# Attention layers of a decoder kernel: the split maxima moved within SBUF instead of through DRAM, and the stacks issued behind them

## The chip, the core and the metric

One core of one Trainium2 chip runs the whole decoder in one launch. The metric is the device time in microseconds (us), median of three runs. The engines are named as the profile names them: PE is TensorE (PEld its weight loads), DVE is VectorE, ACT is ScalarE, POOL is GpSimd, and SP is SyncE, which issues almost all DMAs of this kernel, in the order of one list.

## The reference, cut to what matters

Two decoder layers over `x` of shape (16, 256, 256): attention with rotary positions and a causal mask, cross attention over 120 context rows, an expert layer by product keys, a second self-attention with a band added to its scores, a bidirectional attention flow, and a mixture of experts. The change touches the three attention layers, which all have 16 heads of 16 dims:

```python
scores = jnp.einsum('bhqd,bhkd->bhqk', Q, K) / sqrt(d)      # + causal mask, or + band
probs = jax.nn.softmax(scores, axis=-1)
heads = jnp.einsum('bhqk,bhkd->bhqd', probs, V)
```

## The kernel before

`attention_stage` is one program that is built three times, as `causal`, `cross` and `band`. Each works through 16 batch elements of 256 queries. One batch element is called b, and its 16 heads fall in two halves of 8 (`CH` = 8), named by c = 0 and c = 1.

For each b the stage does this. The projections of queries and keys are made in four jobs (`project`, j = 0 to 3: queries and keys of half 0, then of half 1). Each result is split into three bf16 parts that sum to the fp32 value. SP writes the parts to DRAM (`qscratch` L467, three transfers; `kscratch` L470, one) and reads them back laid out by head: one transfer into `qs` (L481) and three into `ks` (L483). These four reads are the **stack** of one half, `stack(b, par, c)`. Six slots of 16 rows, 96 rows in all, let one bf16 matmul give an fp32-like score.

The scores are computed twice. `find` (L584) makes them with queries on the partitions, and DVE takes each query's negated maximum (`nmax`, L840 or L843). When the 8 heads of a half are found, `turn_max(b, par, c)` transposes the maxima on PE (L598); ACT copies them (L713, L714); POOL splits them into three bf16 parts with three operations (L769, L770, L772, the last signals `n_ready`). SP stores the parts in DRAM (L489), waits for the landing, and reads them into rows 96 to 98 of `qs` (L491). `head` (L608) makes the scores again with keys on the partitions, and these three rows, times ones in `ks`, subtract the maximum in the same matmul. ACT applies exp (L707, `probT`), PE multiplies by the values (L628), ACT copies the result to `oq` (L723), and SP gathers `oq` into `oqp` with 2 times 4 transfers (L500, in `weigh` with j = 2 and 3). The first copy to `oq` of the next b waits until those gathers have landed. Row sums, reciprocals and the output projection follow (L639, L861, L864, L645, L871, L655, L880).

Every engine walks the same written order, `macro(e, b, par)` (L330): a loop over s = 0 to 15, in which `head(b, s)` and `find(b + 1, s)` go side by side, and the other work has fixed places. A macro therefore works on b (heads), b + 1 (find, values), b + 2 (turn, project, stack of half 0) and b - 1 (sums, out). What concerns the change:

- at s = 0, after `head(b, 0)`: `stack(b + 1, 1)`, then `turn_max(b, 1)`, and at the end of the step `find(b + 1, 0)`
- at s = 2: the second gather of b - 1 (`weigh` with j = 3), and projection 0
- at s = 8: `stack(b + 2, 0)`, then projection 2
- at s = 9: `turn_max(b + 1, 0)`, after `find(b + 1, 9)`
- at s = 11: projection 3; at s = 14: the first gather of b

`stack` exists on SP alone; the other engines pass over it. PE's `find` of head 0 or 8 waits until the stack of its half has landed (`stacked[c]`), and PE's `head` 0 or 8 waits for the maxima of its half (`n_in[c]`). So `find(b + 2, 0)`, at the start of the next macro, needs the stack issued at s = 8, and `head(b + 1, 0)`, just before it in PE's order, needs the maxima sent at s = 9. Between these two on PE stands the transpose L598 of `turn_max(b + 1, 1)`.

Of the kernel before, what the change touches and what calls it, by code (L numbers as in the profile page):

```python
# [11 lines left out]
BF16 = mybir.dt.bfloat16  # L12
# [4 lines left out]
B, S, D = 16, 256, 256  # L17
# [10 lines left out]
def wait(eng, sem, value):  # L28

    if isinstance(value, int) and value <= 0:  # L30
        return
    eng.wait_ge(sem, value)
# [20 lines left out]
class Room:  # L53
# [12 lines left out]
    def sb(self, name, shape, dt=F32):  # L66
        return self.ctx.enter_context(self.nc.sbuf_tensor(f"{self.stage}_{name}", shape, dt))
# [4 lines left out]
    def sem(self, name):  # L72
        self.sems.append(self.nc.alloc_semaphore(f"{self.stage}_{name}"))
        return self.sems[-1]
# [104 lines left out]
def attention_stage(nc, kind, stats, ident, d, ahead, context):  # L179
# [19 lines left out]
    CH = HEADS // DC  # L199
# [7 lines left out]
    ROWS = 6 * HD  # L207
# [11 lines left out]
    with ExitStack() as ctx:  # L219
        r = Room(nc, ctx, kind)  # L220
        stats.open(r)
        sb, ps, sem = r.sb, r.ps, r.sem
# [36 lines left out]
        qs = sb("qs", [P, 2, HEADS, S], BF16)  # L259
# [5 lines left out]
        npart = sb("npart", [CH, 2, 3, S], BF16)  # L265
# [5 lines left out]
        warm = sb("warm", [P, 1])  # L271
        qscratch = nc.dram_tensor(f"{kind}_qscratch", (2, DC, 6, P, S), BF16).ap()
        kscratch = nc.dram_tensor(f"{kind}_kscratch", (2, DC, 3, P, KS), BF16).ap()
        nscratch = nc.dram_tensor(f"{kind}_nscratch", (2, 2, 3, CH, S), BF16).ap()

        ps_p = ps("ps_p", [P, 2, 512])
        ps_1 = ps("ps_1", [P, 2, 512])
# [20 lines left out]
        n_taken = sem("n_taken")  # L298
        n_rest = sem("n_rest")
        n_ready = sem("n_ready")  # L300
        n_out = sem("n_out")
        n_in = [sem(f"n_in{c}") for c in range(DC)]
        s2_done = sem("s2_done")
        p_ready = sem("p_ready")
# [16 lines left out]
        def there(b):  # L321

            return 0 <= b < B


        PROJECT, OUT, VALUES, STACK = (2, 5, 8, 11), 13, 15, 8
        WEIGH, SUMS, NORMALISE, MOMENTS, NORM = 6, 4, 7, 3, 4
        MOVES = 16 * HEADS // 2

        def macro(e, b, par):  # L330

            for s in range(HEADS):
                e.head(b, par, s)
                if s > 0:
                    e.factor(b, par, s - 1)
                if s == 0:
                    if there(b + 1):
                        e.stack(b + 1, 1 - par, 1)
                    if there(b - 1):
                        e.turn_max(b, par, 1)  # L340
                if there(b - 1):
                    if s == WEIGH - 4:
                        e.weigh(b - 1, 1 - par, NQUAD - 1)
                    if s == SUMS:
                        e.sums(b - 1, 2 * b + 2)
                    if s == SUMS + 1:
                        e.sums_end(b - 1)
                    if s == NORMALISE:
                        e.normalise(b - 1, 1 - par)
                if s >= WEIGH and s % 4 == WEIGH % 4:  # L350
                    e.weigh(b, par, (s - WEIGH) // 4)
                if s == NORM and there(b + 3):
                    e.norm(b + 3)
                if there(b + 2):
                    if s == 1:
                        e.turn(b + 2, par)
                    if s == 2:
                        e.bias(b + 2)
                    if s == STACK:
                        e.stack(b + 2, par, 0)  # L360
                    if s in PROJECT:
                        e.project(b + 2, par, PROJECT.index(s))
                if s == OUT and there(b - 1):
                    e.out(b - 1)
                if s == MOMENTS and there(b - 2):
                    e.moments(b - 2)
                if there(b + 1):
                    if s == VALUES:
                        e.values(b + 1, 1 - par)
                    e.find(b + 1, 1 - par, s)  # L370
                    if s == CH + 1:
                        e.turn_max(b + 1, 1 - par, 0)
            e.factor(b, par, HEADS - 1)
            e.end()

# [52 lines left out]
        def _(sp):  # L428
# [25 lines left out]
            def settle(sem, value):  # L454


                wait(sp, sem, value)
                sp.wait_ge(weights, 16 * nload)

            class Sync(Part):  # L460
# [25 lines left out]
                def turn_max(self, b, par, c):  # L486

                    settle(n_ready, 2 * b + c + 1)
                    sp.dma_start(nscratch[par, c].rearrange("a h t -> h a t"), npart[:, c, :, :]).then_inc(n_out, 16)  # L489
                    settle(n_out, 16 * (2 * b + c + 1))  # L490
                    sp.dma_start(qs[ROWS:ROWS + 3, par, c * CH:(c + 1) * CH, :], nscratch[par, c]).then_inc(n_in[c], 16)  # L491

                def weigh(self, b, par, j):

# [18 lines left out]
        def _(pe):  # L513
# [12 lines left out]
            class Tensor(Part):  # L526
# [73 lines left out]

                def head(self, b, par, h):
                    if h % CH == 0:
                        pe.wait_ge(n_in[h // CH], 16 * (b + 1))

                    wait(pe, p_ready, HEADS * b + h - 1)
                    for k in range(KT):
                        c0, n = kcol[k], S - qfrom[k]
                        mm = nc.tensor.matmul(ps_2[0:KN, h % 2, c0:c0 + n], ks[0:ROWS + 3, par, h, k * KN:(k + 1) * KN],  # L608
                                              qs[0:ROWS + 3, par, h, qfrom[k]:S], start=True, stop=not rope)
                        if rope:  # L610
                            mm = nc.tensor.matmul(ps_2[:, h % 2, c0:c0 + P], ident16[:], mask[:, 1, :],  # L611
                                                  start=False, stop=True)
                    mm.then_inc(s2_done, 1)
# [47 lines left out]
        def _(act):  # L661
# [5 lines left out]
            class Scalar(Part):  # L667
# [41 lines left out]
                def turn_max(self, b, par, c):  # L709
                    act.wait_ge(nt_done, 2 * b + c + 1)  # L710
                    wait(act, n_ready, 2 * b + c - 1)
                    wait(act, n_out, 16 * (2 * b + c - 1))
                    nc.scalar.activation(nfull[:, c, :], ps_n[0:CH, 0:S], ACT.Copy)  # L713
                    nc.scalar.activation(npart[:, c, 0, :], ps_n[0:CH, 0:S], ACT.Copy).then_inc(n_taken, 1)  # L714

# [1733 lines left out]
def decoder(nc, d):  # L2449
    with ExitStack() as ctx:  # L2450
        def sb(name, shape):
            return ctx.enter_context(nc.sbuf_tensor(name, shape, F32))
        stats = Stats(nc, sb)
        ident = sb("ident", [P, P])
        ahead = Ahead(nc, ctx)
        with ExitStack() as early:
            context = Context(nc, early, "early")
            attention_stage(nc, "causal", stats, ident, d, ahead, context)
            attention_stage(nc, "cross", stats, ident, d, ahead, context)
        peer_stage(nc, stats, ident, d, ahead)  # L2460
        last = Last(nc, ctx, "last")
        attention_stage(nc, "band", stats, ident, d, ahead, last)
        route = Route(nc, ctx.enter_context(ExitStack()))
        bidaf_stage(nc, stats, ident, d, route, last)
        moe_stage(nc, ident, d, route)
# [13 lines left out]
```

## Time and profile before

| | us |
|---|---|
| median of 3 runs (3632.45 to 3639.7) | 3635.33 |
| the profiled execution | 3634.44 |
| its span, first to last instruction | 3632.6 |
| causal stage, about | 31 to 511 |
| cross stage, about | 515 to 895 |
| expert layer by product keys, about | 895 to 2392 |
| band stage, about | 2392 to 2830 |

Over the whole span the page of the profile gives PE 89% busy, DVE 72%, POOL 57%, ACT 51%, and a mean granted TensorE clock of 0.948 of full speed. In the 40 slices of the page, the slices 6 to 9 (the cross stage) show PE at 7 to 8 tenths with a clock of 8 to 9 tenths, while causal and band show PE at 8 to 9 tenths with the clock at 9. A row of the timeline reads: start, duration, engine, line, operation, out<-in, and in brackets the idle time of the engine before it with what ended it. Where operations of a kind follow one another, x3 says that three are merged in the row.

### The profile page before, as it was taken

How to read it: one execution, taken by the hardware profiler on the slowest of the kernel's cores; microseconds unless marked ns; L12 is line 12 of the kernel's file. 1: busy time of each engine (PE TensorE's matmuls, PEld its weight loads, DVE VectorE, ACT ScalarE, POOL GpSimd, SP SyncE). 2: the span in 40 equal slices, each digit the busy share in tenths (PEclk: the TensorE clock that was granted, in tenths of full speed). 3: DMA queues.
4: the chain of work that ended last, by engine and by line, in shares of the span. 5: the costliest groups of instructions: out<-in, count | busy, mean ns of one | idle time of the engine just before them, and what ended most of it. 6: DMA issues, size and time to landing. Idle time of an engine off the chain costs nothing. (4 is left out here: it accounts for less than half of the span.)

```text
span 3632.6 us, 95157 instructions
## 1 busy us (share of the span) xinstructions
PE 3238.9 (89%) x33694; PEld 2753.6 (76%) x33695; DVE 2620.0 (72%) x10695; ACT 1834.9 (51%) x4800; POOL 2067.8 (57%) x2454
## 2 busy tenths in 40 slices
PE   5999977876599999999999999978888898899998
PEld 4777754554589999999999999855555686899998
DVE  6666634453899999999999999848888577333333
ACT  1434434543577777777777777726565221222221
POOL 4444435552377777777777777758886232333332
PEclk8999988997799999999999999989999898899999
DMA  5444424442200000000000000035553231566665
GB/s 155 111 118 125 109 66 119 122 116 74 84 2 2 2 2 2 2 2 2 3 2 2 2 3 2 2 82 128 138 131 88 84 100 44 170 185 177 186 176 134
DMA packets 255744, 277.73 MB, mean 76 GB/s; under 512 B 43871, under 2 KB 200287, under 8 KB 254815
## 3 DMA queue, kind: packets, MB, share of 16 engines
q1 hardware_dynamic: 241694, 253.40, 24.1%
q0 software_dynamic: 13632, 18.91, 3.6%
q8 instruction: 245, 4.01, 0.5%
q14 instruction: 173, 1.41, 0.1%
HBM read 187.34 MB, written 72.29 MB: 71 GB/s over the span
## 5 line engine op out<-in xcount | busy, mean ns | idle before, releaser
L1295 POOL TENSOR_TENSOR peer_hot_v<-peer_hot_e,peer_parts 80x512 bf16<-80x512 bf16 x768 | 920.9, 1226 | 271.0 <-DVE peer_hot_e L1338 266.2
L1091 PE MATMUL peer_ps_u<-peer_up,peer_g 128*128 128x256 f32 x2048 | 513.8, 396 | 0.6 <-DVE x_all L1438 0.6
L1072 PEld LDWEIGHTS peer_ps_h<-peer_xnT,peer_down 128*128 128x128 f32 x4096 | 503.9, 195 | 13.6 <-DMA peer_down<-in_peer_down 1.0
L1072 PE MATMUL peer_ps_h<-peer_xnT,peer_down 128*128 128x128 f32 x4096 | 505.9, 278 | 0.7 <-DMA peer_down<-in_peer_down 0.7
L1201 ACT ACTIVATE peer_hot_u<-peer_count,peer_minus_u 80x128 bf16<-80x128 bf16 x1536 | 462.3, 426 | 2.6 <-PE peer_ps_w L1082 1.5
L1082 PE MATMUL peer_ps_w<-peer_hot_v,peer_hot_u 80*128 80x32 bf16 x12288 | 348.3, 177 | 80.9 <-DVE peer_g L1352 36.1
L1091 PEld LDWEIGHTS peer_ps_u<-peer_up,peer_g 128*128 128x128 f32 x2048 | 382.5, 197 | 49.5 <-issue 1.0
L1082 PEld LDWEIGHTS peer_ps_w<-peer_hot_v,peer_hot_u 80*128 80x128 bf16 x12288 | 338.1, 97 | 101.2 <-issue 64.6
L2272 POOL DMA_INDIRECT out<-moe_y,moe_target x71 | 112.5, 1585 | 312.6 <-DVE moe_y L2371 309.6
L1169 ACT ACTIVATE peer_g<-peer_ps_h 128x512 f32<-128x512 f32 x256 | 145.3, 590 | 249.4 <-PE peer_ps_h L1072 249.1
L2216 PE MATMUL moe_ps_t<-moe_xgT,moe_w 128*128 128x128 f32 x2272 | 267.9, 277 | 0.0
L2216 PEld LDWEIGHTS moe_ps_t<-moe_xgT,moe_w 128*128 128x128 f32 x2272 | 262.0, 194 | 0.1
L2226 PE MATMUL moe_ps_y<-route_w,moe_hT 128*128 x1136 | 256.8, 379 | 0.0
L2226 PEld LDWEIGHTS moe_ps_y<-route_w,moe_hT 128*128 128x128 f32 x1136 | 210.5, 190 | 25.7
L1344 DVE TENSOR_TENSOR peer_hot_u<-peer_count,peer_uvT 80x2048 bf16<-80x2048 bf16 x160 | 229.9, 1437 | 0.0
L707 ACT ACTIVATE causal_probT<-causal_ps 128x384 f32<-128x384 f32 x256 | 124.5, 488 | 204.3 <-PE causal_ps L611 201.3
L2252 ACT ACTIVATE moe_hT<-moe_hT 128x512 f32<-128x512 f32 x142 | 89.4, 629 | 229.4 <-DVE moe_hT L2362 229.4
L843 DVE TENSOR_REDUCE band_nmax<-band_ps 128x2 f32<-128x512 f32 x256 | 171.6, 680 | 41.9 <-PE band_ps L584 41.3
L840 DVE TENSOR_REDUCE causal_nmax<-causal_ps 128x1 f32<-128x128 f32 (+1 forms) x512 | 153.0, 349 | 58.2 <-PE causal_ps L588 57.8
L1206 ACT ACTIVATE peer_hot_u<-peer_hot_u,peer_iota 80x2048 bf16<-80x2048 bf16 x96 | 192.2, 2002 | 3.1
L1352 DVE TENSOR_TENSOR peer_g<-peer_ps_w,peer_g 128x512 f32<-128x512 f32 x256 | 173.9, 679 | 11.8 <-PE peer_ps_w L1082 11.8
L707 ACT ACTIVATE band_probT<-band_ps 128x512 f32<-128x512 f32 x256 | 146.9, 593 | 64.2 <-PE band_ps L608 59.9
(373 smaller groups left out, 7235.0 us busy)
## 6 DMA issues: line engine op xcount, KB each, us to landing
moe_w<-in_moe_w SPq DMA_DIRECT2D x142, 512.0 KB, 4.5
causal_qs<-causal_qscratch SPq DMA_DIRECT2D x32, 384.0 KB, 3.9
cross_qs<-cross_qscratch SPq DMA_DIRECT2D x32, 384.0 KB, 3.6
band_qs<-band_qscratch SPq DMA_DIRECT2D x32, 384.0 KB, 4.0
route_w<-in_moe_w SPq DMA_DIRECT2D x8, 1024.0 KB, 6.0
causal_qscratch<-causal_part SPq DMA_DIRECT2D x32, 192.0 KB, 2.7
causal_kscratch<-causal_part SPq DMA_DIRECT2D x32, 192.0 KB, 2.0
causal_ks<-causal_kscratch SPq DMA_DIRECT2D x32, 192.0 KB, 4.2
```

The source lines that it names most:

```text
L707: nc.scalar.activation(probT[0:KN, h, :], ps_2[0:KN, h % 2, 0:COLS], ACT.Exp).then_inc(p_ready, 1)
L843: ins = nc.vector.tensor_reduce(nmax[:, :, h], ps_1[:, h % 2, 0:TT * KS].rearrange("p (q k) -> p q k", q=TT), AX.X, ALU.max, negate=True)
L1072: mm = nc.tensor.matmul(ps_h[:, n % 2, k * P:(k + 1) * P], down[:, c, 4 * n + k, :], xnT[:, par, c, :], start=(c == 0), stop=(c == DC - 1))
L1082: mm = nc.tensor.matmul(ps_w[:, n % 2, k * EV:(k + 1) * EV], hot_u[0:SEL, n % RING, k // 2, :, k % 2], hot_v[0:SEL, n % RING, part, k // 2 ...
L1091: mm = nc.tensor.matmul(ps_u[:], g[:, par, v, :], up[:, v, :], start=(v == 0), stop=(v == EV - 1))
L1201: ins = nc.scalar.activation(hot_u[0:SEL, n % RING, k // 2, :, k % 2], count[0:SEL, :, 0], ACT.Square, bias=minus_u[0:SEL, token:token + 1])
L1206: nc.scalar.activation(flat, flat, ACT.Relu, bias=iota[0:SEL, 1:2], scale=-1.0).then_inc(u_act_ready, 1)
L1295: ins = nc.gpsimd.tensor_tensor(hot_v[0:SEL, n % RING, part], hot_e[0:SEL, n % RING], w, ALU.mult)
L1344: nc.vector.tensor_tensor(hot_u[0:SEL, n % RING], numbers.broadcast_to((SEL, CHUNK // 2, P, 2)), ut, ALU.is_equal).then_inc(u_ready, 1)
L1352: nc.vector.tensor_tensor(gs, ps_w[:, n % 2, :].rearrange("p (k v) -> p v k", v=EV), gs, ALU.mult).then_inc(gw_ready, 1)
L2216: mm = nc.tensor.matmul(ps_h[:, half, m * P:(m + 1) * P], w1[:, par, half, c, m * P:(m + 1) * P], xgT[:, par, c, :], start=(c == 0), stop= ...
L2226: mm = nc.tensor.matmul(ps_y[:, par, 0:D], hT[:, par, m, :], w2[:, ex, m, :], start=(m == 0), stop=(m == HC - 1))
```

## The change

The scratch tensor `nscratch` and the semaphore `n_out` go. The three parts of the maxima are moved by three transfers within SBUF, each from 8 partitions of `npart` (512 bytes each) to one row of `qs`; `n_in[c]` counts three transfers, and ACT's wait before it overwrites `npart` is on `n_in[c]` in place of `n_out`. In `macro`, `turn_max(b, 1)` now stands ahead of `stack(b + 1, 1)` at s = 0, and `stack(b + 2, 0)` moves from s = 8 to the end of s = 10, behind `turn_max(b + 1, 0)`.

```diff
-        PROJECT, OUT, VALUES, STACK = (2, 5, 8, 11), 13, 15, 8
+        PROJECT, OUT, VALUES, STACK = (2, 5, 8, 11), 13, 15, CH + 2
...
                 if s == 0:
+                    if there(b - 1):
+                        e.turn_max(b, par, 1)
                     if there(b + 1):
                         e.stack(b + 1, 1 - par, 1)
-                    if there(b - 1):
-                        e.turn_max(b, par, 1)
...
-                    if s == STACK:
-                        e.stack(b + 2, par, 0)
...
                     if s == CH + 1:
                         e.turn_max(b + 1, 1 - par, 0)
+                if s == STACK and there(b + 2):
+                    e.stack(b + 2, par, 0)
...
                 def turn_max(self, b, par, c):
 
                     settle(n_ready, 2 * b + c + 1)
-                    sp.dma_start(nscratch[par, c].rearrange("a h t -> h a t"), npart[:, c, :, :]).then_inc(n_out, 16)
-                    settle(n_out, 16 * (2 * b + c + 1))
-                    sp.dma_start(qs[ROWS:ROWS + 3, par, c * CH:(c + 1) * CH, :], nscratch[par, c]).then_inc(n_in[c], 16)
+                    for k in range(3):
+                        row = ROWS + k
+                        sp.dma_start(qs[row:row + 1, par, c * CH:(c + 1) * CH, :], npart[:, c, k, :]).then_inc(n_in[c], 16)
...
-                        pe.wait_ge(n_in[h // CH], 16 * (b + 1))
+                        pe.wait_ge(n_in[h // CH], 3 * 16 * (b + 1))
...
-                    wait(act, n_out, 16 * (2 * b + c - 1))
+                    wait(act, n_in[c], 3 * 16 * b)
```

## Rows read from the trace of the kernel before

**Rows 1.** Waits of PE, cross stage: who <- whom: us in total, times, longest

```profile
PE cross_ps L608 <- DMA cross_qs<-cross_nscratch: 35.2, 16, 5.6
PE cross_ps L608 <- ACT cross_probT L707: 10.4, 8, 2.8
```

**Rows 2.** Waits of PE, band stage

```profile
PE band_ps_n L598 <- DVE band_nmax L843: 15.7, 16, 1.0
...
PE band_ps L608 <- DMA band_qs<-band_nscratch: 1.6, 1, 1.6
```

**Rows 3.** Timeline of SP, one macro of the cross stage and the next stack

```profile
718.42 0.29 SPq L489 DMA_DIRECT2D cross_nscratch<-cross_npart  x1
720.11 0.25 SPq L491 DMA_DIRECT2D cross_qs<-cross_nscratch  x1
...
728.50 2.50 SPq L500 DMA_DIRECT2D cross_oqp<-cross_oq  x4
...
734.88 0.32 SPq L481 DMA_DIRECT2D cross_qs<-cross_qscratch  x1
735.25 1.35 SPq L483 DMA_DIRECT2D cross_ks<-cross_kscratch  x3
```

**Rows 4.** Timeline, the same border between two macros

```profile
717.74 0.66 POOL L772 TENSOR_TENSOR cross_npart<-cross_nrest,cross_npart 8x256 bf16<-8x256 f32 x1
...
721.76 0.32 PE L608 MATMUL cross_ps<-cross_qs,cross_ks 99*120 99x256 bf16 x1 [1.28 <-DMA cross_qs<-cross_nscratch]
...
722.14 0.27 PE L584 MATMUL cross_ps<-cross_ks,cross_qs 96*128 96x120 bf16 x2
```

**Rows 5.** Timeline, the first and the last of the 14 such borders

```profile
567.93 0.66 POOL L772 TENSOR_TENSOR cross_npart<-cross_nrest,cross_npart 8x256 bf16<-8x256 f32 x1
...
575.37 0.41 PE L584 MATMUL cross_ps<-cross_ks,cross_qs 96*128 96x120 bf16 x2
...
843.66 0.66 POOL L772 TENSOR_TENSOR cross_npart<-cross_nrest,cross_npart 8x256 bf16<-8x256 f32 x1
...
850.93 0.41 PE L584 MATMUL cross_ps<-cross_ks,cross_qs 96*128 96x120 bf16 x2
```

**Rows 6.** Timeline, one border of the causal stage and one of the band stage

```profile
256.65 0.66 POOL L772 TENSOR_TENSOR causal_npart<-causal_nrest,causal_npart 8x256 bf16<-8x256 f32 x1
...
265.04 0.22 PE L584 MATMUL causal_ps<-causal_ks,causal_qs 96*128 96x128 bf16 x1
...
2600.84 0.81 POOL L772 TENSOR_TENSOR band_npart<-band_nrest,band_npart 8x256 bf16<-8x256 f32 x1
...
2607.91 0.38 PE L584 MATMUL band_ps<-band_ks,band_qs 96*128 96x256 bf16 x2
```

**Rows 7.** View of tile cross_oqp: issue ns min/median/max, start of first and last; landing

```profile
L500 SPq DMA_DIRECT2D cross_oqp<-cross_oq x128: 585/592/733, 573.8 to 892.3; - x128
...
DMA to landing us min/median/max: 1.9/2.0/3.3
```

**Rows 8.** View of tile cross_ks, DMAs: from issue to landing

```profile
DMA to landing us min/median/max: 1.8/3.2/4.2
```

**Rows 9.** View of tile band_ks, DMAs: from issue to landing

```profile
DMA to landing us min/median/max: 2.9/4.2/5.6
```

**Rows 10.** Timeline of the cross stage: single waits of PE and ACT

```profile
554.46 0.47 PE L608 MATMUL cross_ps<-cross_qs,cross_ks 99*120 99x256 bf16 x1 [2.96 <-DMA cross_qs<-cross_nscratch]
...
701.85 0.32 PE L608 MATMUL cross_ps<-cross_qs,cross_ks 99*120 99x256 bf16 x1 [2.28 <-DMA cross_qs<-cross_nscratch]
...
732.45 0.38 ACT L723 ACTIVATE cross_oq<-cross_ps_o 128x256 f32<-128x256 f32 x1 [4.38 <-issue]
...
879.64 0.75 PE L608 MATMUL cross_ps<-cross_qs,cross_ks 99*120 99x256 bf16 x2 [3.00 <-ACT cross_probT L707]
```

**Rows 11.** Windows at the start of two macros, busy us (xcount), PEclk, DMA

```profile
681.00:689.00 8.00, 6.48 (x63) 4.15 (x62) 5.57 (x13) 5.07 (x16) 6.29 (x10) 1.00 0.38 94
702.00:710.00 8.00, 7.42 (x59) 4.59 (x58) 4.00 (x10) 5.19 (x16) 5.32 (x8) 0.79 0.37 98
```

More of the change, by code:

```diff
@@ L273, in attention_stage @@
         kscratch = nc.dram_tensor(f"{kind}_kscratch", (2, DC, 3, P, KS), BF16).ap()
-        nscratch = nc.dram_tensor(f"{kind}_nscratch", (2, 2, 3, CH, S), BF16).ap()
         ps_p = ps("ps_p", [P, 2, 512])
@@ L300, in attention_stage @@
         n_ready = sem("n_ready")
-        n_out = sem("n_out")
         n_in = [sem(f"n_in{c}") for c in range(DC)]
```

## The prediction

> **What bounds the kernel now.** I read the page's slices first, to see which stages the change can touch; then PE's waits in each attention stage; then SP's timeline over one macro, because SP issues every transfer concerned in one fixed order; and last PE and POOL at the border between two macros.
>
> In the cross stage PE's largest wait is for the split maxima: 35.2 us in 16 waits [rows 1]. In the band stage there is one such wait, 1.6 us [rows 2], and causal hardly knows it. So the round trip through DRAM costs time in cross, and the cover elsewhere is PE's and DVE's own work.
>
> The chain at a border of cross is plain in the rows. POOL ends the split at 717.74 + 0.66 = 718.40. SP stores at 718.42, waits, and loads at 720.11 [rows 3]; PE starts head 0 at 721.76, and find 0 at 722.14 [rows 4]. From the split's end to head 0 it is 3.4 us, to find 0 3.7 us. I call this second distance the margin, because everything that SP puts between the split and the landing of the next stack must fit in it once the stack stands behind the maxima. Over the 14 borders of cross the margins run from 3.7 to 7.0 us and sum to 68.3; the first is 575.37 - 568.59 = 6.8, the last 850.93 - 844.32 = 6.6 [rows 5]. In band the typical margin is 2607.91 - 2601.65 = 6.3 (5.9 to 6.9, sum 86.7 over 14), in causal 265.04 - 257.31 = 7.7 [rows 6].
>
> **The change, part by part.**
>
> *Maxima within SBUF.* Removed per half: one store, SP's wait, one load, 720.11 - 718.42 = 1.7 us and again 721.76 - 720.11 = 1.65 us from issue to use [rows 3, 4]. Added: three transfers. The trace has none of this form. For the issue, the low bound is the 0.25 us of the load L491, the high bound 0.59 us of the gather, the only transfer here from SBUF to SBUF, which has twice the partitions [rows 3, 7]. The same tile's store takes 0.29 us [rows 3], so I stay near it with 0.33 us, which makes 1.1 us for three with their gaps (bounds 0.9 and 1.9). For the landing I take the gather's 2.0 us [rows 7], bounds 1.65 and 3.3. The last maximum is then in place 0.8 + 2.0 = 2.8 us after the split instead of 3.4: 0.6 us saved at head 0, more at the borders where SP was late.
>
> *The stack of half 0 behind the maxima.* This is the largest term. Before, the stack is issued at s = 8, at 734.88 in one macro, and four transfers later all is there before find 0 asks for it: PE has next to no wait on it. Afterwards it starts only when the split is done and the three transfers are issued. It needs 1.3 us from its first issue to its fourth (735.25 plus two thirds of 1.35, less 734.88) [rows 3], and the fourth lands 3.2 us later in cross, 4.2 us in band and, by the same view, in causal [rows 8, 9]. So find 0 comes at 0.0 + 1.1 + 1.3 + 3.2 = 5.6 us after the split in cross, and 6.6 us in band and causal. Against the margins: cross 14 x 5.6 - 68.3 = +10.1 us; band 14 x 6.6 - 86.7 = +5.7 us; causal nothing, 7.7 covers 6.6. The cover in causal is PE's own six heads; it is gone only if the sum passes 7.7. In the band stage the wait adds to PE's wait for DVE before L598, up to 1.0 us, which ends just before find 0 [rows 2], and the one 1.6 us wait for maxima is inside the band sum already.
>
> What queues behind the moved stack on SP: the transfer of projection 3 and the first gather. They are issued some 0.8 us later than now; the gather is waited for only half a macro later, so this costs nothing.
>
> *The maxima of half 1 ahead of the stack of half 1.* SP no longer sits in the store's wait, but the stack's four issues (1.9 us) now stand between the maxima and the second gather: 1.1 + 1.9 = 3.0 us from the split to the gather, against 2.4 to 4 before. Alone this is nothing. But head 0 and with it the transpose of half 1 no longer come just ahead of find 0, but 2.8 us ahead of it, so measured from find 0 the second gather is issued some 2 to 3 us earlier. Now it is issued at 728.50 and ACT, idle for 4.38 us, takes up its copy at 732.45 [rows 3, 10]. In 8 places this reaches PE, 10.4 us in all [rows 1]. I book all 10.4 as gained in cross. Band and causal have ACT waits of this kind that never reach PE in a full macro.
>
> *The clock.* The window after a wait of 2.28 us at the border [rows 10] shows a granted clock of 0.79, so part of it at 1.2 GHz, and 59 matmuls in 7.42 busy us; the same window of a macro that began after a wait of 1.3 us, like that of [rows 4], shows 1.00, 2.4 GHz throughout, and 63 in 6.48 [rows 11]. The same 63 at 0.79 would take 7.9 us: 1.4 us more. After the change PE waits about 3 us at every border of cross (0.9 for head 0, 2.2 for find 0). By the same view five of its macros start at full clock now; if all five fall, 5 x 1.4 = +7.0 us.
>
> *Start and tails.* The first head 0 of cross waits 2.96 us [rows 10]; there the stack is early in either order, and the next wait, find 0's own stack, lands 1.5 us ahead of today's start, so -1.5. In the last macro of causal and cross nothing but the gather's issue counts (PE waits 3.00 us through ACT [rows 10]); SP reaches it 1.1 instead of 1.7 us after the split: -0.6 each, less 0.1 for the macro before. Together -1.1.
>
> *A rule of the Trainium skill.* The gathers are four small transfers issued back to back in 2.50 us, and each lands 2.0 us after its own issue [rows 3, 7]: their fixed times overlap, and only the issues add up. The Trainium skill, DMA: Bandwidth & Descriptors, section Rules for kernel authors, says to coalesce many small transfers, since below 64 KB one pays mostly overhead. If each of the three 4 KB moves paid its overhead in turn, the maxima would arrive at 3 x 2.0 = 6.0 us, 0.4 us behind the stack, and cross would lose another 5.6 us. By the rows I leave that out.
>
> *Sum.* +10.1 + 5.7 - 10.4 + 7.0 - 1.5 - 1.1 = +9.8 us. On the profiled execution's 3634.44 us (span 3632.6 plus 1.8 around it) this gives 3644.2; the median of the runs shown lies 0.9 higher, so 3645 us.
>
> **The rivals.**
>
> *No change worth measuring.* The stack may land sooner in its new place, where SP has no writes right behind it. With issues of 0.25 to 0.3 us and the fastest stacks (3.0 instead of 3.2 us, 3.9 instead of 4.2), find 0 comes at 5.2 in cross (+4.5) and 6.1 in band (about 0); with -10.4 + 7.0 - 2.6 that is -1.5, 3634 us. For it: the difference to my terms is 0.4 us per border. Against it: band has 0.3 us to give before it loses.
>
> *The new transfers issue like the gather.* At 0.59 us each, 1.9 us for three: 6.4 us in cross (+21.3), 7.4 in band (+16.9), causal still covered at 7.4 of 7.7. With -10.4 + 7.0 - 2.6 this is +32, 3667 us. For it: the gather is the only SBUF to SBUF row. Against it: it has 16 partitions and rows of 1 KB, and the same tile's own store takes 0.29.
>
> *Faster: the second gather sets the length of cross's macros.* From one border to the next it takes (844.32 - 568.59) / 13 = 21.2 us [rows 5], 4.9 of them margin and 16.3 from find 0 to the split. If the early gather frees ACT, and PE keeps 1.00 at the starts, those 16.3 lose the 1.4 us of slow clock or of ACT's wait, one of which every macro has: 15.0. With 5.4 at the border the macro is 20.4, 14 x -0.8 = -11 us; band at 6.5 is +4.3, start and tails -2.6: -9.5, 3626 us. It decides from the point at which the clock stays up: a border wait of 1.3 us leaves it, one of 2.3 does not, so it needs a border well below the 3 us that I expect. That is the weak spot of this rival, and its chance is in my not having proven where the clock falls.
>
> That the maxima gain nothing is no rival of its own: head 0 could come as late as 5 us after the split, and find 0 would still wait for the stack.
>
> **How the numbers follow.** A measurement of this kernel can tell about 0.2%, 7.3 us, from no change. Forecast (3645, own range 3638 to 3657): 0.45, of which 0.06 lie within 7.3 us. No change (3634): 0.23, all within. Slow issue (3667): 0.14. Faster (3626): 0.18, of which 0.02 lie within. Slower: 0.39 + 0.14 = 0.53; same: 0.06 + 0.23 + 0.02 = 0.31; faster: 0.16. The range of 8 in 10 leaves half of the fastest case and a bit over half of the slowest out: 3626 to 3663.
>
> **What the changed profile would show.** PE's wait for the maxima at L608 in cross falls from 35 us to about 12 or less, and a new wait for `cross_ks<-cross_kscratch` or `cross_qs<-cross_qscratch` at L584 takes its place, about 2 us each at 14 borders, some 30 us. In band the same wait appears with 0.2 to 0.8 us, and PE's wait for DVE at L598 stays. Causal shows neither. From the split's end to find 0 I expect 5.6, 6.6 and 7.7 us in cross, band and causal. SP's three issues show 0.33 us each. ACT's idle time before L723 falls from over 4 us to under 3, and PE's 10.4 us on `cross_probT` nearly go. More of the windows at the start of a macro show 0.79. The forecast is wrong if find 0 does not wait for the stack, if the stack lands under 3.9 us after its first issue in cross, or if the clock at the macro starts is 1.00.

## The result and the profile after

The changed kernel takes 3713.68 us (median of 4 runs, 3713.37 to 3722.2), the kernel before 3636.97 beside it on the same chip. The ratio is 1.0218, 95% interval 1.0204 to 1.0232: 77 us slower. The forecast was 3645 us with a range of 3626 to 3663, so the sign was right and the size was wrong by 69 us, outside the range. The profiled execution of the changed kernel took 3722.2 us; its span is 3720.4, against 3632.6. It is the longest of the four, 8.5 us above the other three, so what is read from its trace adds up to 88 us and not to 77.

Lines after the edit are two lower than before: `find` is L582, `head` L606, the stack L479 and L481, the gather L498, and L489 is now one of the three transfers within SBUF.

PE's waits in the cross stage of the changed kernel, the view of [rows 1]:

```profile
PE cross_ps L582 <- DMA cross_ks<-cross_kscratch: 45.3, 14, 4.6
PE cross_ps L606 <- DMA cross_qs<-cross_npart: 21.1, 16, 2.8
...
PE cross_ps L606 <- ACT cross_probT L705: 4.7, 3, 3.4
```

The wait for the maxima fell from 35 to 21 us. A wait of 45 us in 14 places, for the stack of find 0, is new. Of the 4.7 us for ACT 3.6 lie in the last macro, after its head 0 at 915 us. [rows 1] leave that macro out; before, it has this line (869 us on):

```profile
PE cross_ps L608 <- ACT cross_probT L707: 3.5, 3, 3.0
```

Up to the last head 0, the stretch of [rows 1], the wait for ACT fell from 10.4 to 1.4 us. In the band stage (2480 to 2780 us), the view of [rows 2], the wait for the stack appears at every macro but the first:

```profile
PE band_ps L582 <- DMA band_ks<-band_kscratch: 16.7, 10, 2.2
PE band_ps_n L596 <- DVE band_nmax L841: 10.9, 11, 1.0
...
PE band_ps_o L626 <- issue: 9.1, 11, 0.9
```

One border of the cross stage in the changed kernel's timeline, which answers to [rows 3, 4]. Columns: start us, us, engine, line, operation, and in brackets the idle time before it:

```profile
698.22 0.66 POOL L770 TENSOR_TENSOR cross_npart<-cross_nrest,cross_npart 8x256 bf16<-8x256 f32 x1
...
698.91 2.11 SPq L489 DMA_DIRECT2D cross_qs<-cross_npart  x3
...
701.12 0.38 SPq L479 DMA_DIRECT2D cross_qs<-cross_qscratch  x1
701.54 1.35 SPq L481 DMA_DIRECT2D cross_ks<-cross_kscratch  x3
702.19 0.32 PE L606 MATMUL cross_ps<-cross_qs,cross_ks 99*120 99x256 bf16 x1 [1.22 <-DMA cross_qs<-cross_npart]
...
703.47 2.64 SPq L498 DMA_DIRECT2D cross_oqp<-cross_oq  x4
...
705.62 0.38 PE L582 MATMUL cross_ps<-cross_ks,cross_qs 96*128 96x120 bf16 x2 [2.89 <-DMA cross_ks<-cross_kscratch]
```

The split ends at 698.88. The three transfers stand on SP for 2.11 us, the stack starts 2.24 us after the split, its last issue ends at 702.89, and find 0 comes at 705.62: 6.7 us after the split. Three things are to be seen: the transfers take SP twice as long as I had said, head 0 no longer sets the border, and PE stands still twice in it, for 1.22 and for 2.89 us. The view of line L489 gives the issue over all 96 transfers of a stage (ns, min/median/max):

```profile
L489 SPq DMA_DIRECT2D cross_qs<-cross_npart x96: 623/689/712, 561.5 to 920.0; - x96
L489 SPq DMA_DIRECT2D band_qs<-band_npart x96: 623/689/1461, 2477.9 to 2895.3; - x96
```

**By stage.** To split the 87.8 us between the spans I take in each stage the time from the first head 0 to the last head 0 (15 macros), and within it the border (split to find 0, 14 of them) and what is left, mostly find 0 to the next split (the mean of the 13 stretches that lie between two of these borders). All from the starts and ends of these instructions, as in [rows 5, 6].

```
us                  head 0 to head 0    border, mean    find 0 to split
                    before   after      before after    before after
causal              417.6    427.4      7.6    8.0      20.7   20.7
cross               314.7    350.2      4.9    7.2      16.5   16.8
band                365.5    407.6      6.2    8.1      18.3   19.5
```

The differences are +9.8, +35.5 and +42.1, together 87.4 of the 87.8: starts and tails give nothing. 14 borders make 14 x 7.17 - 68.3 = +32.1 in cross, 14 x 8.11 - 86.7 = +26.8 in band and 14 x (7.96 - 7.63) = +4.6 in causal. So nearly three quarters of the loss (63.5 us) are the borders, and the largest thing outside them is in band, 13 x 1.15 = 15 us between find 0 and the split. Of causal's other 5 us, 3.1 lie between find 0 of the last batch element and its split.

**The clock in band.** That last part is TensorE's clock, as far as rows side by side can show it. Two neighbouring macros of the changed kernel, 10.5 us each from find 0 on (us of the window, busy us (xcount) of PE, PEld, DVE, ACT, POOL, PEclk, DMA share, GB/s):

```profile
2535.50:2546.00 10.50, 9.67 (x87) 6.38 (x88) 9.81 (x18) 5.87 (x13) 9.11 (x16) 1.00 0.53 129
2561.40:2571.90 10.50, 9.78 (x60) 6.03 (x60) 5.51 (x13) 5.66 (x12) 5.98 (x10) 0.70 0.40 92
```

In the first, find 0 had waited 1.5 us, the clock stays at 1.00, and the next split comes 17.8 us after find 0. In the second it had waited 1.76 us:

```profile
2561.44 0.61 PE L582 MATMUL band_ps<-band_ks,band_qs 96*128 96x256 bf16 x2 [1.76 <-DMA band_ks<-band_kscratch]
```

The granted clock is 0.50, 1.2 GHz, from just before that find 0 until between 2567 and 2568 us, 60 matmuls are done where the other macro does 87, and the split comes after 20.7 us. The whole stretches from find 0 to the next split show the same 139 matmuls in three lengths, here one of each:

```profile
2535.47:2553.25 17.78, 16.50 (x139) 11.15 (x140) 16.58 (x32) 12.29 (x27) 14.96 (x26) 1.00 0.44 112
2700.04:2719.39 19.35, 18.07 (x139) 11.68 (x140) 16.23 (x32) 12.71 (x27) 14.97 (x26) 0.91 0.37 102
2561.44:2582.15 20.71, 19.44 (x139) 12.64 (x140) 15.29 (x32) 12.72 (x27) 14.68 (x26) 0.85 0.37 95
```

and one from the kernel before:

```profile
2632.49:2650.79 18.30, 16.49 (x141) 11.12 (x139) 16.11 (x33) 12.88 (x29) 15.73 (x27) 1.00 0.58 139
```

Of the 13 stretches after, two are at full clock and take 17.8 us, seven take 19.3 to 19.4, and four take 20.3 to 20.7. The 13 before are all at full clock. At full clock the changed kernel is 0.5 us faster than the 18.3 before, because PE waits less at the matmul with the values (L628 before, L626 after: 18.0 us over the 13 stretches before, 10.6 after). So the slow clock costs about 22 us in these 13 stretches, and the shorter wait gives 7 back. No run here kept the wait before find 0 and took away the slow clock; the rows show that they come together.

Over the long windows the clock falls in all three stages; after:

```profile
94.00:495.00 401.00, 368.83 (x3608) 287.70 (x3607) 260.07 (x762) 160.25 (x377) 156.34 (x240) 0.99 0.42 110
580.00:915.00 335.00, 246.94 (x1804) 162.39 (x1802) 148.87 (x347) 152.14 (x467) 154.28 (x257) 0.85 0.40 101
2500.00:2880.00 380.00, 321.78 (x2460) 208.33 (x2460) 279.78 (x573) 208.41 (x446) 273.75 (x476) 0.93 0.45 113
```

and before, the same stretches of the stages:

```profile
93.00:485.00 392.00, 365.16 (x3613) 287.32 (x3611) 260.55 (x764) 161.62 (x380) 156.27 (x240) 1.00 0.44 113
560.00:870.00 310.00, 244.99 (x1876) 161.53 (x1876) 155.02 (x361) 153.52 (x492) 160.26 (x268) 0.91 0.43 113
2455.00:2800.00 345.00, 303.85 (x2521) 203.49 (x2522) 287.78 (x584) 206.12 (x454) 278.69 (x484) 1.00 0.49 125
```

### The profile page after: what moved, and what is told of

The parts are those of the page before. It is cut to its first block and busy times, and to the rows that moved or that the text cites. A ratio compares the mean times of both kernels' runs of the same rounds, so it can differ in the third digit from the quotient of the medians.

```text
span 3720.4 us, 95157 instructions
## 1 busy us (share of the span) xinstructions
PE 3278.4 (88%) x33694; PEld 2768.4 (74%) x33695; DVE 2615.1 (70%) x10695; ACT 1846.7 (50%) x4800; POOL 2067.8 (56%) x2454
## 5 line engine op out<-in xcount | busy, mean ns | idle before, releaser
L1080 PE MATMUL peer_ps_w<-peer_hot_v,peer_hot_u 80*128 80x32 bf16 x12288 | 348.4, 177 | 79.7 <-DVE peer_g L1350 35.5
L841 DVE TENSOR_REDUCE cross_nmax<-cross_ps 128x2 f32<-128x240 f32 x256 | 97.5, 399 | 155.7 <-PE cross_ps L582 154.3
```

The source lines that it names most:

```text
L841: ins = nc.vector.tensor_reduce(nmax[:, :, h], ps_1[:, h % 2, 0:TT * KS].rearrange("p (q k) -> p q k", q=TT), AX.X, ALU.max, negate=True)
L1080: mm = nc.tensor.matmul(ps_w[:, n % 2, k * EV:(k + 1) * EV], hot_u[0:SEL, n % RING, k // 2, :, k % 2], hot_v[0:SEL, n % RING, part, k // 2 ...
```

## The experiments

The change has two parts, the transfers and the order; e1 and e2 take one each. Each ratio is against the kernel before in the same session. That kernel took 3631.9 to 3632.9 us in these and 3637.0 beside the changed kernel, so a difference of two times from different sessions is good to about 5 us.

**e1: the order alone.** The kernel before, with the three edits of the order and the maxima still through DRAM:

```diff
-        PROJECT, OUT, VALUES, STACK = (2, 5, 8, 11), 13, 15, 8
+        PROJECT, OUT, VALUES, STACK = (2, 5, 8, 11), 13, 15, CH + 2
# and turn_max(b, par, 1) ahead of stack(b + 1, 1 - par, 1)
```

> The kernel before with the new order alone: the stacks stand behind the maxima on SP, and the maxima still go through DRAM. Theory O (the order costs the time, since find 0 now waits for a stack that is issued only after the split): SP reaches the stack's first issue about 2.1 + 0.3 us after the split (store's wait and load), about as late as with the three transfers of the changed kernel, so find 0 comes at about 7.0 us after the split in cross and 8.0 in band, and the time is 3690 to 3720 us. Theory T (the new transfers cost the time wherever they stand): 3637 us, as before.

3693.57 us, ratio 1.0168 (1.0145 to 1.0191). The order by itself costs 62 us, as theory O had it. Its borders are a half us shorter than expected, 6.5 us in cross and 7.5 in band: SP issues the stack 1.8 us after the split, behind the store's landing and the load. In the changed kernel it is 2.2 us, behind three transfers within SBUF.

**e2: the maxima alone.** The changed kernel with the old order.

```diff
-        PROJECT, OUT, VALUES, STACK = (2, 5, 8, 11), 13, 15, CH + 2
+        PROJECT, OUT, VALUES, STACK = (2, 5, 8, 11), 13, 15, 8
# and stack(b + 1, 1 - par, 1) ahead of turn_max(b, par, 1) again
```

> The changed kernel with the old order: three transfers within SBUF, stacks ahead of the maxima. Theory O: the three issues (2.1 us) and a landing of 1.4 us after them replace a chain of 3.4 us, so 3628 to 3643 us, no wait of find 0 for a stack. Theory T: 3700 us or more.

3621.46 us, ratio 0.9971 (0.9961 to 0.9980): 10 us faster than before. So the two parts don't add: -10 and +62 apart, +77 together. Find 0 doesn't wait for a stack in any of the 14 borders of a stage. With the new order, the transfers' issue, which costs nothing in e2, stands ahead of the stack and holds it 0.4 us longer than the round trip does in e1. And in band three of the 13 stretches from find 0 to the split hold a part at 1.2 GHz in e1, eleven in the changed kernel.

**e3: one transfer instead of three.** The changed kernel with only the high part moved; the rows of the two lower parts stay zero, so that part of the maximum's precision is left out.

```diff
-                    for k in range(3):
+                    for k in range(1):
```

> The changed kernel with one of the three transfers; the middle and low parts of the maxima are left out (their rows hold zeros). SP's time between the split and the stack falls from 2.1 to 0.7 us. Theory O with the issue time as the size of the loss: find 0 at about 5.5 us after the split in cross and 6.4 in band, where the clock stays at 1.00 again: 3640 to 3655 us. Theory O without the issue time (any place behind the split is as bad): 3700 us or more. Theory T, in proportion: 3662 us.

3673.39 us, ratio 1.0115 (1.0098 to 1.0132). 40 us less than the changed kernel, by 1.4 us less of issue per half: the two issues are worth about half of the loss. But I had expected 3640 to 3655; the time lies between the numbers of the theories. The borders came near what was expected (cross 5.5 us, band 6.7 against 6.4), the rest of a band macro did not: find 0 to split is 19.5 us against 18.3 before, 15 us over 13 stretches. I had also expected the clock in band at 1.00, and it is not:

```profile
2640.00:2780.00 140.00, 120.61 (x961) 78.85 (x961) 118.71 (x228) 80.36 (x178) 107.09 (x187) 0.96 0.45 115
```

Five of the 13 stretches hold a part at 1.2 GHz, and these five take 9 of the 15 us more. The other eight are at full clock and take 19.1 us against 18.4 in the same places before. Six of those eight have one DVE multiplication of 2.3 to 2.9 us, where the usual one takes 0.29, while POOL runs one instruction behind the other. It is one of the two in the second row here:

```profile
2556.40 0.67 POOL L771 TENSOR_TENSOR band_npart<-band_nrest,band_npart 8x256 bf16<-8x256 f32 x1
2556.62 2.87 DVE L855 TENSOR_TENSOR band_probT<-band_probT,band_band 128x130 f32<-128x130 f32 x2
2557.03 0.87 POOL L754 TENSOR_TENSOR band_probT<-band_probT,band_band 128x130 f32<-128x130 f32 x2
2557.87 1.26 POOL L762 TENSOR_TENSOR x_all<-x_all,band_bo 128x512 f32<-128x512 f32 x1
```

Of these 256 multiplications 14 take over 0.9 us in e3, 3 before, and 8 in the changed kernel. The Trainium skill, GPSIMD Engine Reference, Key points, says that POOL shares its SBUF interfaces with DVE and that DVE instructions with two SBUF inputs contend with it. The row would agree with that, but most of the 256 take 0.29 us, and no run here took POOL's work away, so the cause of the slow ones stays open.

**e4: the transfers by themselves.** The kernel before, with seven kinds of transfer issued by SP, each alone and waited for, three times over, at the end of the causal stage where hardly anything else is moved. It ran once and took 3655.89 us, 24 us more than the kernel before where I had expected 50; only the issues are of interest.

```diff
+                for n in range(3):
+                    sp.dma_start(prb[0:1, 0:8, :], one).then_inc(probe, 16)
+                    ...
+                    sp.dma_start(nscratch[0, 0, 0], one).then_inc(probe, 16)
+                    ...
+                    sp.dma_start(prb[32:33, 0:8, :], nscratch[0, 0, 0:1]).then_inc(probe, 16)
+                    ...
+                    sp.dma_start(prb[96:97, 0:8, :], prb[0:1, 0:8, :]).then_inc(probe, 16)
```

> The kernel before, with seven forms of a small transfer issued one at a time at the end of SP's list of the causal stage, each awaited, in three passes: 8 partitions to one SBUF row (the change's form), 8 partitions to 8 partitions within SBUF, the same with 3 x 512 bytes each, 8 partitions to DRAM, DRAM to one row, DRAM to 3 rows (the form before), one row to one row. If going from SBUF to SBUF makes the issue long, all SBUF to SBUF forms take 0.6 to 0.7 us and those with DRAM 0.24 to 0.3. If the single destination row does, only the forms to one row take long. If it was SP's traffic around them, the first form takes 0.3 us here. The time is about 50 us above the kernel before.

The views of the lines, issue in ns (min/median/max): L520 is 8 partitions into one row, as in the change; L523 8 into 8; L526 all three parts, 8 into 8; L529 the store; L532 a load into one row; L538 one row into one row of SBUF.

```profile
L520 SPq DMA_DIRECT2D causal_prb<-causal_npart x3: 664/674/735, 508.9 to 532.0; - x3
L523 SPq DMA_DIRECT2D causal_prb<-causal_npart x3: 645/645/678, 510.8 to 533.8; - x3
L526 SPq DMA_DIRECT2D causal_prb<-causal_npart x3: 624/625/633, 512.6 to 535.6; - x3
L529 SPq DMA_DIRECT2D causal_nscratch<-causal_npart x3: 269/273/283, 514.5 to 537.5; - x3
L532 SPq DMA_DIRECT2D causal_prb<-causal_nscratch x3: 221/221/221, 515.7 to 538.7; - x3
L538 SPq DMA_DIRECT2D causal_prb<-causal_prb x3: 556/556/582, 518.6 to 541.8; - x3
```

The DMA share is 0.02 there, and no engine computes in the second and third pass. The median issue is still 0.56 to 0.67 us whenever both ends lie in SBUF, whatever the shape, and 0.22 to 0.27 us when one end is DRAM. It is neither the single row nor traffic. The three parts in one transfer (L526) cost as much as one part. No run has moved all three parts to their rows of `qs` in one transfer.

**e5 and e6: the order, one half at a time.** Both have the maxima within SBUF. e5 has only half 1 in the new order, e6 only half 0.

```diff
# e5, against e2
-                    if there(b + 1):
-                        e.stack(b + 1, 1 - par, 1)
                     if there(b - 1):
                         e.turn_max(b, par, 1)
+                    if there(b + 1):
+                        e.stack(b + 1, 1 - par, 1)
# e6, against the changed kernel: the same lines the other way
```

> The maxima moved within SBUF, half 0 in the old order (its stack of keys and queries stands ahead of the maxima's transfer), and half 1 in the new one. Theory (the cost of the order is find 0 of the next block, which waits for the stack of half 0): half 1's stack isn't needed until find 8, so this stays at the 3621 us of the kernel with both halves in the old order, 3617 to 3630. Rival (each half's stack that starts 2 us later costs as much, by what is queued behind it on SP and by find 8): half of the 93 us between that kernel and the changed one, 3660 to 3670.

> The maxima moved within SBUF, half 0 in the new order and half 1 in the old one: the other half of the split. Theory (find 0 waits for half 0's stack): nearly the whole of the 93 us, 3700 to 3715. Rival (both halves cost): 3660 to 3675.

e5: 3654.03 us, ratio 1.0069 (1.0054 to 1.0083). e6: 3705.15 us, ratio 1.0207 (1.0192 to 1.0222). Against e2's 3621 the halves cost 33 and 84 us, and both together 92. Find 0's half is most of it: e6 came out as the theory had it. But the theory gave half 1 nothing, and that is wrong; e5 lies 24 us above its range and 6 below the rival's. In e5 the band's border is 6.0 us (6.2 in e2), and find 0 to split goes from 18.3 to 19.5. ACT's timeline in one such macro:

```profile
2622.10 0.60 ACT L705 ACTIVATE band_probT<-band_ps 128x512 f32<-128x512 f32 x1
2627.67 0.38 ACT L721 ACTIVATE band_oq<-band_ps_o 128x256 f32<-128x256 f32 x1 [4.97 <-issue]
```

and SP's:

```profile
2618.05 2.09 SPq L489 DMA_DIRECT2D band_qs<-band_npart  x3
2620.24 0.38 SPq L479 DMA_DIRECT2D band_qs<-band_qscratch  x1
2620.67 1.35 SPq L481 DMA_DIRECT2D band_ks<-band_kscratch  x3
2622.12 2.61 SPq L498 DMA_DIRECT2D band_oqp<-band_oq  x4
```

ACT's copy to `oq` waits until the gather L498 of the b before has landed (the row names no releaser; e10 puts it to the test). The gather stands behind the wait for the split, the three transfers and the stack, and ends at 2624.73. In e2 the stack uses the time before the split (there SP issues it at 2596.54 and the maxima at 2599.79), and the gather starts 7.0 us after head 0 instead of 8.8.

**e10 and e11: the gather first.** e5 and the changed kernel, with the stack of half 1 behind the gather too.

```diff
-                    if there(b + 1):
-                        e.stack(b + 1, 1 - par, 1)
...
+                if s == WEIGH - 4 and there(b + 1):
+                    e.stack(b + 1, 1 - par, 1)
```

> As e5 (half 1 in the new order, 3654 us), but the stack of half 1 stands behind the gather of the weighted values as well, so that this gather is issued some 2 us earlier in each block. Theory (half 1's new order costs because the gather stands behind the wait for the split, the three issues and the stack's issues, and ScalarE's copy of the next weighted values, with the exponentials behind it, waits for the gather): ScalarE's idle time before that copy falls from 4.7 us in the band layer to 2.5 or less, and the time returns to 3612 to 3630. Rival (half 1's stack itself is late for find 8): it gets later still, 3655 to 3680.

> The changed kernel (3714 us) with the same edit: both halves in the new order, half 1's stack behind the gather. Theory (two costs that partly overlap: find 0 waits for half 0's stack, and ScalarE's copy waits for the gather): the second cost goes, 3670 to 3698, below the 3705 us of half 0 alone, since there too the gather started later (8.6 us after head 0 in the cross layer against 6.6 with neither half moved). Rival (find 0's wait alone sets the changed kernel's time and the gather hides behind it): 3705 to 3718.

e10: 3684.61 us, ratio 1.0146 (1.0132 to 1.0161), slower than e5 and just above the rival's 3655 to 3680. Its wait at ACT went as expected: the idle time before the first copy to `oq` is 1.8 us in band, from 4.7. But now find 8 waits for its stack, which was the rival; find 0 waits for no stack in e10. PE's waits in band (2500 to 2780 us), e5:

```profile
PE band_ps L606 <- ACT band_probT L705: 8.8, 11, 1.4
```

and e10:

```profile
PE band_ps L582 <- DMA band_ks<-band_kscratch: 19.1, 10, 2.6
```

So both mechanisms are there, one on each side: neither of the two places behind the split that were tried suits the stack of half 1, ahead of the gather (e5) or behind it (e10). e11: 3715.54 us, ratio 1.0225 (1.0211 to 1.0239), no change from 3714, the rival's number. ACT's idle time before the copy fell again, from 1.6 to 1.0 us in band and from 1.1 to 0.2 in cross, and brought nothing, while find 8 came to wait 3.0 us in cross and 4.6 in band. So the gather hides behind find 0's wait, or its gain went into find 8's; e11 does not part the two.

**e7 and e8: the transfers issued by POOL.** POOL issues them itself behind its last split operation; e7 in the old order, e8 in the new one, where SP still waits for the split and then issues the stack at once.

```diff
+                    pool.wait_ge(n_ready, 2 * b + c + 1)
+                    for k in range(3):
+                        row = ROWS + k
+                        pool.dma_start(qs[row:row + 1, par, c * CH:(c + 1) * CH, :], npart[:, c, k, :]).then_inc(n_in[c], 16)
```

> The maxima moved within SBUF by transfers that POOL issues itself behind the split, instead of SP; the stacks in the old order. SP is relieved of 6 issues of 0.6 to 0.7 us in each block, POOL gets them. Theory (in the old order SP's issues stand where nothing waits): no change against the 3621 us with them on SP, 3615 to 3627, as long as an issue on POOL takes less than 1 us. Rival (POOL is needed for the next split and for the bias, and 4 us more of it in each block come back through the heads): 3640 or more.

> The new order without the transfers' issue ahead of the stack: SP waits for the split as in the changed kernel and then issues the stack at once, since POOL issues the three transfers. Theory (the cost is the time by which the stack comes later, wait and issue together): the stack starts 2.1 us earlier than in the changed kernel and find 0 with it, cross margin from the split to find 0 near 5.1 us (7.2 in the changed kernel), time 3650 to 3675. Rival 1 (the three issues are all of the cost): at or under 3632, the kernel before. Rival 2 (the wait is the cost whatever stands behind it): 3690 to 3715.

e7: 3689.41 us, ratio 1.0160 (1.0144 to 1.0176). e8: 3723.15 us, ratio 1.0254 (1.0233 to 1.0275). Both missed as totals, because of band: POOL has a part of band's multiplications (L750 here), and PE waits for it, 53 us between 2480 and 2780:

```profile
PE band_ps_o L623 <- POOL band_probT L750: 53.1, 20, 3.4
```

In cross, where POOL has room, they say more. From the first head 0 to the last it takes 299.1 us in e7 and 328.7 in e8: waiting for the split before the stack costs 30 us there even with no issue between. With the 2.1 us of issue it is 350.2, another 21. But the 30 us come in another way than in the changed kernel. PE's waits in cross (560 to 880 us), e8:

```profile
PE cross_ps L603 <- DMA cross_qs<-cross_npart: 42.3, 15, 4.5
```

e8's stack is issued 0.03 us after the split and lands after 4.9, but the maxima let head 0 start only after 5.0 (3.3 in e7), and find 0 comes at 5.5. In both runs POOL issues them at the same time after the split; their median landing is 2.0 us in e7 and 3.6 in e8, where the stack's four transfers are under way. So in e8 the maxima and the stack are late together, and it doesn't price the stack's wait alone.

**e9: what gained, put together.** The old order, the maxima within SBUF, issued by POOL in causal and cross and by SP in band (`if kind != "band"` around the lines of e7).

> The old order with the maxima moved within SBUF, the three transfers issued by POOL in the causal and the cross layer and by SP in the band layer. From the profiles of the kernels with all of them on SP and all on POOL: the cross stage took 701.1 and 686.1 us, the causal one 515.5 and 507.9, the band one was 84 us longer on POOL. So if the stages do not act on each other, 3621.5 - 15.0 - 7.6 = 3599, range 3592 to 3606. Rival (part of the cross stage's gain was moved into the next stage, work ahead of time for it): 3608 to 3621.

3603.47 us, ratio 0.9920 (0.9906 to 0.9935): 29 us faster than before, 18 faster than e2, 110 faster than the changed kernel. That is in the expected range, but with luck. Causal ends at 515.5 us in e2 and at 507.9 in e7, cross at 889.8 and 874.3, so all that was gained up to the end of cross is 15.5 us, causal's 7.6 among them. The expectation's 15.0 for cross is nearly all of that, and it takes off causal's 7.6 once more; without that the sum is 3606. And of the 18.6 us between the profiled executions of e2 and e9 only 8.3 lie between the first and the last head 0 of the three stages. Beside `cross_qs<-cross_npart`, PE's waits in cross now end on DVE:

```profile
PE cross_ps L608 <- DMA cross_qs<-cross_npart: 19.8, 17, 4.0
PE cross_ps L584 <- DVE cross_nmax L849: 18.0, 14, 1.6
```

## Why the prediction was wrong

The step that failed is the border: "find 0 comes at 0.0 + 1.1 + 1.3 + 3.2 = 5.6 us after the split in cross, and 6.6 us in band and causal". The mechanism is right, find 0 waits for the stack at every border. Means over the 14 borders, from the split:

```
us                        cross              band
                          said   measured    said   measured
stack's first issue       1.1    2.23        1.1    2.28
its last issue begins     2.4    3.59        2.4    3.64
lands, find 0             5.6    7.1         6.6    8.1
```

- *The issue, 0.33 us each.* Measured 0.69. I stayed "near" the same tile's store [rows 3] and put the gather [rows 7] down as different in shape; e4 shows that the shape doesn't matter and both ends in SBUF do. Even the high bound, 0.59, was too low. The issue carries 1.1 of the 1.5 us of each border; 14 x 1.1 in each of cross and band is 31 us of the 78 by which the profiled execution missed (69 by the medians). e3 confirms the size: with one transfer the stack is issued at 0.85 us and cross's border is 5.5 us.
- *The landing.* 3.5 and 4.4 us instead of 3.2 and 4.2: 14 x (0.3 + 0.2) = 7 us more. That the stack lands sooner in a quiet place, as the rival of no change had it, is wrong.
- *Causal, booked at nothing.* Its cover was 7.7 us, the stack lands at 7.9: the stage lost 9.8 us, 4.6 of them at the borders. Such a stage sits at the edge: 1.3 us more than said were enough.
- *The clock in band, not booked at all.* I had asked that question for cross alone (+7.0). The border in band cost more than its own length, 15 us net and some 22 by the slow clock, behind waits of 1.5 to 2.6 us that I had put at "0.2 to 0.8". In cross the time at 1.2 GHz between find 0 and the split grew by 25 us over the 13 stretches, at half speed 12.5 us of full clock lost; I estimate its cost at 11 to 12 us where I had booked 7.
- *The gather, -10.4 us.* Half right. It is issued 1.8 us earlier counted from find 0 (4.6 instead of 6.4 us in cross), ACT's idle time before the copy fell from 3.8 to 1.1 us, and PE's wait for ACT fell from 10.4 to 1.4 us up to the last head 0. PE's idle time between find 0 and the split fell by 7.5 us over the 13 stretches of cross. That is the gain; the clock took more back, and the stretches grew by 5 us. Counted from head 0 the gather came 1.5 us later (8.4 instead of 6.8), and that count decides once find 0 is on time, as e5 shows.
- *Start and tails, -2.6.* Nothing: the stages' middles already hold 87.4 of 87.8 us.
- *Together.* Against the +9.8 that was said: borders of cross and band 43 us, the rest of band 15, causal 10, the rest of cross 7, start and tails 3.
- *Which macros are slow.* I counted five macros of cross that start at full clock; in windows of 8 us from head 0 it is six. Two of them began after waits of 2.07 and 2.16 us, so "1.3 leaves it, 2.3 does not" was weaker than it looked.
- *The rule of the Trainium skill (DMA: Bandwidth & Descriptors, Rules for kernel authors) on small transfers.* Leaving it out was right: the three maxima do not pay their overhead in turn. They are issued 0.7 us apart, and head 0 runs 3.4 us after the split in cross, not 6.0. The overhead came back on the issuing engine's side: three transfers hold SP for 2.1 us, where all three parts in one held it for 0.63 (L526 in e4).

Of the rivals "the new transfers issue like the gather" was nearest, 3667 us. It names the right cause, and misses by 47 for the other points. The chance of slower, 0.53, was the right side; the range was too narrow above, because each further term (clock, landing, causal's cover) goes the same way once the border grows, and I had let them vary apart.

Left open: why one DVE multiplication in most band macros of e3 takes 2 to 4 us, and why some band macros keep the full clock behind a wait of 1.5 us and others don't.

## What to carry to other kernels

A wait put at the head of a DMA queue's list costs what stands behind it, so write down for each transfer behind it by when it must be issued. Before, the stack had landed 3.5 us ahead of find 0 in cross, 5.2 in band and 6.6 in causal, on average; the new order issues it 5.3, 6.9 and 6.7 us later. Find 8 and ACT's copy had less to give: in e10 and e5 they were late too. Issue costs of a queue depend on where both ends lie: the round trip through DRAM took SP 0.5 us of issue (and 1.4 us of waiting between), the "shorter" way within SBUF 2.1 us of issue. The engine that makes the data can issue its transfer, if it has room, and the room differs from stage to stage (e7 against e9). And where a wait can lower TensorE's clock, price it in every stage whose border grows, not just in the one that shows it now.

## What the runs showed of the hardware that was not expected

- SP needs 0.56 to 0.73 us to issue a transfer from SBUF to SBUF and 0.22 to 0.28 us when DRAM is at one end, with next to nothing else running (e4). POOL needs 0.52 us for the same transfer that takes SP 0.69. The view of tile `cross_npart` in e7:

```profile
L771 POOL DMA_DIRECT2D cross_qs<-cross_npart x96: 518/521/543, 543.4 to 852.9; - x96
```

- From the start of the issue to SP's next instruction behind the wait, e4 took 1.8 us within SBUF, 1.24 us for the store and 1.3 to 1.6 us for the loads: within SBUF is the slowest of the three per transfer, though faster than the store and the load together.
- The three small transfers of the maxima, issued by POOL in cross, land after 2.0 us (median) in e7 and 3.6 in e8, where the stack is issued at the same moment; only the places of the stacks differ between the two.
- In band, waits of 1.5 us and of 1.8 us before find 0 lay on two sides: full clock behind the one above, and 1.2 GHz for some 6 us beside and behind the other. Neither is a threshold; other waits of 1.5 us in that stage also had a slow stretch behind them.
